# A gated delta-rule layer with experts on one core: all five queues of the recurrence in a new order, with the moves of the queries' rows on another queue

## The reference

```python
q = _short_conv(x @ Wq, conv_q)      # four taps, then silu; k and v alike, k and v three times a token
beta = 2.0 * sigmoid(x @ Wb);  g = -exp(A_log) * softplus(x @ Wa + dt_bias)
q = _l2norm(q) * d ** (-0.5);  k = _l2norm(k)
def step(S, inp):                    # one token
    S = S * exp(gt)
    for i in range(3):
        kS = ki @ S
        S = S + bi * outer(ki, vi - kS)
    return S, qt @ S
o = o * rsqrt(mean(o * o, -1) + 1e-05) * rms_weight * silu(x @ Wg)
return o @ Wo
```

## Time and profile before

| | |
|---|---|
| median of three runs | 4964.96 us |
| the profiled execution | 4958.13 us, span 4956.3 us |
| loop over the blocks, from the first `squares` to the last | 120.4 to 3935.7 us |
| experts, from the first load for them | 4003.8 us to the end |
| busy: PE, PEld, DVE, ACT, POOL | 85%, 76%, 74%, 66%, 33% |
| mean granted clock of TensorE | 0.930 |

### The profile page before, as it was taken

One profiled execution on the slowest core, in us unless ns is written; L12 is line 12 of the kernel. 1 busy time (PEld: TensorE's weight loads), 2 busy tenths in 40 slices (PEclk: granted clock), 3 DMA queues, 4 the chain that ended last, 5 costly groups with the idle time before them and its releaser, 6 DMA issues. The chain is left out here.

```text
span 4956.3 us, 130457 instructions
## 1 busy us (share of the span) xinstructions
PE 4191.2 (85%) x47876; PEld 3757.1 (76%) x47876; DVE 3656.1 (74%) x10194; ACT 3277.9 (66%) x9028; POOL 1648.1 (33%) x1615
## 2 busy tenths in 40 slices
PE   2889888888888888988988889999988866599992
PEld 0888887778787777877887878888887745488882
DVE  6888887878887788878788778888888822344446
ACT  3778776777776677777777777777777711255552
POOL 3434333333333333333333333444433302200004
PEclk6999999999999999999899999999999988699996
DMA  6232232223222233222223222232233123366664
GB/s 235 68 95 72 65 79 74 79 61 89 79 69 65 62 76 72 70 70 86 63 65 86 70 69 82 76 93 66 72 78 83 49 85 119 120 239 233 228 232 140
DMA packets 307816, 485.00 MB, mean 98 GB/s; under 512 B 38784, under 2 KB 252800, under 8 KB 288384
## 3 DMA queue, kind: packets, MB, share of 16 engines
q1 hardware_dynamic: 249488, 432.84, 29.6%
q10 hardware_dynamic: 51568, 27.04, 1.8%
q0 software_dynamic: 6144, 16.79, 1.1%
HBM read 352.02 MB, written 107.75 MB: 93 GB/s over the span
## 5 line engine op out<-in xcount | busy, mean ns | idle before, releaser
L1087 DVE SCALAR_TENSOR_TENSOR conv_acc<-bank,conv_sb,conv_acc 128x256 f32<-128x256 f32 x2688 | 1270.3, 477 | 238.5 <-ACT conv_acc L898 225.3
L646 PE MATMUL bank<-x_cur,w_cur 128*128 128x259 f16 (+1 forms) x6144 | 891.9, 283 | 31.2 <-DVE v_rows L1075 26.3
L1279 POOL TENSOR_TENSOR squares<-kq_t 128x768 f32<-128x768 f32 x128 | 187.8, 1468 | 1868.6 <-ACT kq_t L909 1868.6
L956 ACT ACTIVATE invt<-bank 128x256 f16<-128x256 f32 x1280 | 512.0, 400 | 353.6 <-issue 324.1
L1146 DVE CAST_PREDICATED xs_lev<-mask,bank 128x256 f16<-128x256 uint16 x1536 | 657.1, 428 | 116.7 <-PE bank L710 104.5
L947 ACT ACTIVATE inv<-bank 128x256 f16<-128x256 f32 x1536 | 608.5, 396 | 133.6 <-PE bank L722 130.4
L646 PEld LDWEIGHTS bank<-x_cur,w_cur 128*128 128x128 f16 (+1 forms) x6144 | 570.3, 100 | 117.3 <-DVE v_rows L1075 27.2
L734 PE MATMUL bank<-invt,xs_lev 128*128 128x64 f16 x5120 | 370.2, 196 | 267.8 <-ACT invt L956 263.8
L734 PEld LDWEIGHTS bank<-invt,xs_lev 128*128 128x128 f16 x5120 | 284.1, 99 | 306.9 <-issue 288.6
L898 ACT ACTIVATE conv_acc<-bank,conv_sb 128x256 f32<-128x256 f32 x896 | 426.4, 476 | 132.8 <-PE bank L646 126.4
L778 PE MATMUL bank<-w_sol,k_rows 128*128 128x128 f32 x2048 | 477.8, 317 | 9.5 <-ACT w_sol L966 5.9
(11 more groups left out here) (241 smaller groups left out, 10698.5 us busy)
## 6 DMA issues: line engine op xcount, KB each, us to landing
w_cur<-w_parts_scratch SPq DMA_DIRECT2D x128, 1024.0 KB, 10.7
ew<-e_parts_scratch SPq DMA_DIRECT2D x117, 896.0 KB, 6.3
x_cur<-x_parts_scratch SPq DMA_DIRECT2D x128, 259.0 KB, 7.2
x_slots<-no_rows SPq DMA_DIRECT2D x128, 256.0 KB, 10.8
e_parts_scratch<-e_pair SPq DMA_DIRECT2D x96, 224.0 KB, 7.8
o_rows<-w_sol ACTq DMA_DIRECT2D x512, 32.0 KB, 5.0
y_scratch<-y_buf SPq DMA_DIRECT2D x128, 128.0 KB, 10.7
y_in<-y_scratch SPq DMA_DIRECT2D x32, 512.0 KB, 4.1
```

The lines of the kernel that those rows point to most:

```text
L646: last = mm(bank[i % 2][:, 0:PW], w_cur[k.i % 2][:, wp, kt, c * P:(c + 1) * P].bitcast(BF16 if wp else F16), x_cur[k.i % 2][:, xp, kt, 0:P ...
L956: a(half(dst, l, 1), packed(halves(LEVTT), l), ACT.Copy).then_inc(tt_kept.sem, 1)
L1087: v.scalar_tensor_tensor(acc, bank[at % 2][:, i:i + TB], conv_sb[:, k.h, c, i:i + 1], acc, ALU.mult, ALU.add).then_inc(tap_step.sem if i < ...
```

## The change

The bodies of PE, ACT, DVE, POOL and SP are all written in a new order, and the tables of the semaphores follow. The loop now works with eight stages (k[0] to k[7]) in place of five. The compute engines use k[0] to k[4]; stages 5 and 7 serve SP, which now has a body of its own in the same form.

- `move_outputs` is issued by SP and no longer by ACT. `w_sol` gets a third buffer.
- SP's body is: moves, then loads, then the clear and the store of outputs, then the pieces. The load waits only for the last projection of the block two before it.
- On ACT, `square_outputs` now stands a body later than the moves.
- `mask4` is gone; DVE reads `mask_sb` with a broadcast over the four chunks.
- Some waits stand one step later in the chain: the one for `fix` is now at `solve` (was `from_state`), the one for the values' rows at `right_side`, the one for the keys' rows at `update`.

```diff
-STAGES = 5
-STORED = 5
+R_W = 3
+R_O = 2
+STAGES = 8
...
-            mask4 = sb("mask4", [P, LEVELS, 4, P], F16)
...
-            w_sol = ring("w_sol", 2, [P, UN, P], F32)
+            w_sol = ring("w_sol", R_W, [P, UN, P], F32)
...
+                    def load(k):
+                        b = k.i % (B * H) // H
+                        done(sp, projected, 7, k.n - 2)
...
+                    def move_outputs(k):
+                        done(sp, sol_kept, 7, k.n)
+                        at_least(sp, scaled, k.n + 1 - R_O)
+                        for c in range(4):
+                            sp.dma_start(o_rows[k.i % R_O][c * CH:(c + 1) * CH], w_sol[k.i % R_W][96:128, c::4, :])\
+                                .then_inc(moved[k.i % 2], 16)
...
+                    def store(k):
+                        sp.dma_start(clear_rows[k.n * P:(k.n + 1) * P, :], no_rows[:]).then_inc(cleared, 16)
+                        done(sp, rows_kept, "outputs", k.n)
+                        sp.dma_start(y_dram[k.n], y_buf[k.i % 2][:]).then_inc(stored[k.i % 2], 16)
...
-                    load(0, 0, 0)
-                    for n in range(NIT):
-                        tb, head = n // (B * H), n % (B * H)
-                        if n + 1 < NIT:
-                            load_next(tb, head)
-                        outputs(tb, head)
-                        pieces(tb, head)
+                    def body(k):
+                        move_outputs(k[5])
+                        load(k[0])
+                        store(k[7])
+                        pieces(k[1])
...
                     def from_state(c, k):
-                        if c % 4 == 0:
-                            done(pe, x_kept, ("fix", c // 4), k.n)
-                            done(pe, rows_kept, ("keys", c // 4), k.n, ("values", c // 4))
                         if c == 0:
+                            done(pe, silu_done, 0, k.n)
...
                     def solve(c, k):
+                        if c % 4 == 0:
+                            done(pe, x_kept, ("fix", c // 4), k.n)
...
-                        keep_t(4, 0, k1)
-                        move_outputs(k3)
-                        keep_tt(4, 0, k1)
...
+                        keep_tt(5, 0, k[2])
+                        square_outputs(k[4])
+                        silu(0, k[1])
...
-                    for l in range(LEVELS):
-                        v.tensor_copy(mask4[:, l], mask_sb[:, l, None, :].broadcast_to([P, 4, P]))
```

More of the change, by code:

```diff
@@ L545, in run_bodies @@
                 for i in range(NIT + STAGES - 1):
-                    body(*blocks(i))
+                    body(blocks(i))
             def halves(b):
@@ L776, in update @@
                     def update(c, k):
+                        if c % 4 == 0:
+                            done(pe, rows_kept, ("keys", c // 4), k.n)
                         done(pe, sol_kept, c, k.n)
-                        mm(chain(k), k_rows[k.i % R_ROWS][:, c], w_sol[k.i % 2][:, c], start=True, stop=True).then_inc(upd_made.sem, 1)
+                        mm(chain(k), k_rows[k.i % R_ROWS][:, c], w_sol[k.i % R_W][:, c], start=True, stop=True).then_inc(upd_made.sem, 1)
                     @at_stage
@@ L965, in keep_w @@
                         done(act, sol_made, c, k.n)
-                        a(w_sol[k.i % 2][:, c], chain(k), ACT.Copy).then_inc(sol_kept.sem, 1)
-                    @at_stage
-                    def move_outputs(k):
-                        done(act, sol_kept, 7, k.n)
-                        at_least(act, scaled, k.n - 1)
-                        for c in range(4):
-                            act.dma_start(o_rows[k.i % 2][c * CH:(c + 1) * CH], w_sol[k.i % 2][96:128, c::4, :]).then_inc(moved[k.i % 2], 16)
+                        a(w_sol[k.i % R_W][:, c], chain(k), ACT.Copy).then_inc(sol_kept.sem, 1)
                     @at_stage
@@ L980, in square_outputs @@
                         for i in range(2):
-                            last = a(o_sq[:, i], o_rows[k.i % 2][:, i], ACT.Square, accum_out=o_sum[:, i:i + 1])
+                            last = a(o_sq[:, i], o_rows[k.i % R_O][:, i], ACT.Square, accum_out=o_sum[:, i:i + 1])
                         last.then_inc(o_squared, 1)
@@ L1304, in scale_outputs, with piece @@
                         done(pool, rows_made, "outputs", k.n - 1)
-                        tt(o_norm[:], o_rows[k.i % 2][:], rstd[:, :, None].broadcast_to([P, 2, P]), ALU.mult).then_inc(scaled, 1)
-                    def piece(e, c):
+                        tt(o_norm[:], o_rows[k.i % R_O][:], rstd[:, :, None].broadcast_to([P, 2, P]), ALU.mult).then_inc(scaled, 1)
+                    @at_stage
+                    def piece(k):
+                        e, c = k.tb, k.i % (B * H) - 1
+                        if not 0 <= c < 12:
+                            return
                         i = c % 2
@@ L1316, in piece, with body @@
                         tt(e_pair[i][:, 1].bitcast(BF16), e_raw[i][:], e_pair[i][:, 0].bitcast(F16), ALU.subtract).then_inc(e_low, 1)
[L1318 to L1333 removed]
+                    def body(k):
+                        spread_decay(0, k[1])
+                        spread_decay(1, k[1])
+                        minus_one(0, k[1])
+                        scale_outputs(k[4])
+                        minus_one(1, k[1])
+                        g_rows(k[0])
+                        piece(k[0])
+                        low(1, k[1])
+                        low(0, k[1])
+                        square(k[0])
+                        square_q(k[1])
+                    run_bodies(body)
         attention_scope.close()
```

561 lines of the change are left out of this document (269 added, 292 removed).

## The result

The changed kernel takes 4631.33 us, the median of four runs (4629.74 to 4647.12), beside 4961.89 us for the kernel before in the same comparison (4945.15 to 4970.04). The ratio is 0.9345, with a 95% interval of 0.9313 to 0.9377. The profiled execution of the changed kernel is the longest of its four: 4647.12 us, with a span of 4645.2.

The account below looks back on a forecast made before the run. PE's 25.9 us of work was to bound the body; with 0.9 of small waits and 0.2 for the clock, 27.0 against 30.04. Over 127 bodies plus masks that saves 388: 4570, plus 6.8 to the median, 4577 us; range 4470 to 4940.

Parts of the forecast that it names:

- The waits behind the moves: PE's waits at level_tt and residual behind ACT's four issues: 2.5 us of a 28.32 us full-clock body, leaving 25.8.
- The clock: PE's falls to half clock in the loop, costing 1.5 us a body, become rare without 2 us gaps; 0.2 allowed.
- The moves on the loads' queue: On SP, moves ready at t0 (last projection's end) + 7.3, landed at 14.3, read at 17.0: no wait.
- The free SP: SP has issued loads, clear, store and a piece 4.5 to 5.5 us after t0, and is ready for the moves.
- The store of y: Store issued behind the load, lands before gated_outputs reuses y_buf, 2.4 us late in slow stretches; taken at 0, upper 1.
- The masks and the broadcast: Seven mask copies ahead of the loop go, saving 1.5 us once; DVE's broadcast reads cost nothing.
- The small waits: Remaining small waits of DVE on PE in the loop: 0.9 us on PE's 25.9, giving 26.8 a body.
- the drain: More stages may lengthen filling and draining of the loop by up to 8 us; taken at 0.
- The first rival: Waits only move: PE loses elsewhere in many small waits, body 28.3 us without clock falls, 4744 us; chance 0.20.

Follow-up runs that it names:

- e10: Kernel before, old order, without the four moves and ACT's wait for them, o_rows filled once with a constant; 4523.43 us, ratio 0.9095.
- e1: Kernel before in its old order, with only the four moves issued by SP behind the pieces in place of ACT; 5384.54 us, ratio 1.0839.
- e2: Kernel after in its new order, with only the four moves issued by ACT again; 5092.65 us, ratio 1.0251 to the kernel before.
- e6: Kernel before in its old order, with only one of the four moves issued and waited for; 4972.58 us, ratio 1.0038.
- e4: Kernel after with both first_level instructions moved from DVE to POOL; 4499.25 us, ratio 0.9058 to the kernel before.
- e5: Kernel after with first_level moved to POOL and c_n computed ahead of keep_fix(0) on DVE; 4480.46 us, ratio 0.9034 to the kernel before.
- e3: Kernel after with the level 0 mask copied out once ahead of the loop, so first_level reads no broadcast; 4658.85 us, ratio 0.9386 to the kernel before.
- e7: Kernel after with first_level on POOL, c_n early on DVE, and SP's store ahead of its load; 4448.80 us, ratio 0.8973 to the kernel before.

## Why the prediction was right, and which term was off

- **The waits behind the moves: right.** Both rows are gone, the clock is 1.00 in the loop, and e10, which takes both waits out of the old order, has a body of 26.61 by the mean, 26.10 in the window shown, against 25.8.
- **The clock: right.** 0.2 us a body was allowed, 0 came. In e1, e2 and e6, PE's waits of up to 7.4, 3.4 and 4.9 us come with clocks of 0.86, 0.94 and 0.91; after, PE's waits in the table stay below 1 us. The two go together here, but not always: in the earlier trace rows PE has a gap of 2.1 us, and the clock of that stretch is 0.98.
- **The moves on the loads' queue: right.** Rows ready at t0 + 7.3 forecast, 7.7 measured; last issue at 9.3 forecast, the fourth ending at 10.9 measured (four in 3.10 us); read at 17.0, 18.5 measured. They land 3.0 us after issue, less than the 5.0 taken. That fits a burst that is nearly out by then (the page of the kernel after has 10.4 us for the weights' landing, issued at t0 + 0.6), as the prediction argued. e1 shows what stands on the other side.
- **The free SP: right, but with less margin than I took.** SP was ready at t0 + 6.8, not 4.5 to 5.5, since the issue of y takes 3.52 us where the earlier trace rows had 1.79. The change didn't cause that: the earlier trace rows is a quick block, and I read one where a median was to be had. The tile `y_scratch` from 300 to 3500 us, before:

```profile
L577 SPq DMA_DIRECT2D y_scratch<-y_buf x106: 430/3287/3938, 305.8 to 3480.0; - x106
```

and after:

```profile
L589 SPq DMA_DIRECT2D y_scratch<-y_buf x116: 952/3265/3886, 321.4 to 3480.1; - x116
```

  With 0.9 us more, SP would have held the moves.
- **The store of y: right for this kernel**, 1.3 us in 73 bodies. It became a wait once the body was shorter (e4, e5).
- **The masks and the broadcast: right.** 1.5 forecast, 1.4 less up to the first `squares`, and e3 for the broadcast.
- **The small waits: the mis-sized term.** The prediction put 0.9 us of waits on a floor of 25.9 set by PE, 26.8 in all, and took DVE's 24.9 us as given. Measured are 26.9 us of DVE and 0.6 beside it, 27.44, and PE's 25.9 bounds nothing: e7 has a body below it. The term is 0.6 us too small; the 0.2 allowed for the clock and not needed hid a third of that, which is luck. DVE's own work was taken from the old order, and a duration that depends on what stands beside it does not move with its instruction. The earlier trace rows show two groups that happened to read a bank; the tile `first`, with 284 to 722 ns in the old trace, would have shown the spread, and so would `c_n`, with 156 to 1248.
- **The rest of the 54 us.** In the profiled executions, the forecast is missed by 77 us: 56 in the loop (127 x 0.44), 6.6 in the drain, which was taken at 0 with an upper end of 8, and 13.6 in the experts. The experts are outside the change, and the last two are not its doing as a whole. From the last `squares` to the end, the kernel before takes 1020.6 us in its profiled execution and the kernel after 1040.8, but two runs in the old order take as long: e6 1049.3 and e10 1042.1. From the last `squares` to the first load of the experts' large weights (`ew`) the granted clock is 0.83 before, 0.78 after, 0.78 in e6 and 0.79 in e10. What brings it down there is open.

The first rival, that the waits only move, had the right idea, that the new order has its own faults, but the wrong size and place: one engine's instructions grew by 2.1 us a body, and the largest new wait of PE, 1.3 us a body, is for one of them.

## What to carry to other kernels

Taking the DMAs off an engine's queue paid here only with a list that asks for their data later: the body is 33.3 with the new queue alone, 30.8 with the new order alone, and 27.4 with both, so look for the read before you move the issue. Before you take an engine's busy time over into a new order, look at min and max of each instruction's duration; one with a wide spread may be waiting inside, as `c_n` and `first` were, and its place beside the other engine is part of its price. When DVE is the bound, see which of its instructions have two SBUF operands and lie beside POOL's work, and move those away, to POOL itself if it has room.

## What was not expected of the hardware

- A DVE instruction with two SBUF operands stood still until POOL's running instruction ended: 8 columns took 0.92 us and not 0.16; 256 columns of 16 bits 1.2 and not 0.28. Such standing counts as busy time, so that DVE looked full at 98%.
- SP's fourth DMA, counted from the load of x on, mostly takes some 3.3 us to issue, whichever it is: the store of y before and after (medians 3.29 and 3.27), the store of a piece in the block of e7 shown (3.32). The three ahead of it take 0.4 to 0.6 in the block of the kernel after. SP is held for that long, and all that stands behind it.
- The moves, 32 KB each and issued 7.8 us and more after the loads of x and of 1 MB of weights began on the same queue, landed in 3.0 us; the store of y, 128 KB and issued 1.75 us after, in 10.2. In e7, where the store goes ahead of the loads, it lands in 3.3.
